# Loading the shifted replica in one transfer of 128 partitions, and laying out halves on even and odd partitions

## The reference, cut to what matters

```python
qkv = einsum('oc,bchw->bohw', w_qkv, x)                   # 256 -> 768 channels
y   = conv(qkv, w_dw, 5x5, pad 2, one group per channel)  # depthwise
agg = einsum('gok,bgkhw->bgohw', w_pw, y.reshape(B, 96, 8, H, W))
ms  = concatenate([qkv, agg], 1)                          # heads of 8 q, 8 k, 8 v channels
q, k = relu(...), relu(...)                               # v1: v with a row of ones appended
vk  = einsum('bhdn,bhen->bhde', v1, k)
out = einsum('bhde,bhen->bhdn', vk, q); out = out[:, :, :-1] / (out[:, :, -1:] + 1e-15)
out = einsum('oc,bchw->bohw', w_proj, out)
out = batchnorm(out) * gamma + beta + x                   # over all images and pixels
```

## Time and profile before

| | us |
|---|---|
| median of 3 runs | 2576.74 |
| lowest, highest | 2573.13, 2585.85 |
| the profiled execution | 2585.7 |
| its span | 2583.9 |

### The profile page before, as it was taken

The page is one execution under the profiler, slowest core; times in us unless marked ns, Lnnn a source line. Parts: engine busy times, 40 slices in busy tenths (PEclk is TensorE's granted clock), DMA queues, the critical chain, the costliest instruction groups (busy, mean ns, idle before and its releaser), DMA issues. The chain is left out here.

```text
span 2583.9 us, 36219 instructions
## 1 busy us (share of the span) xinstructions
PE 2282.2 (88%) x13760; PEld 1642.4 (64%) x13760; DVE 856.9 (33%) x1340; ACT 913.0 (35%) x1957; POOL 213.8 (8%) x207
## 2 busy tenths in 40 slices
PE   7999899996978999799979989998998999999730
PEld 6888888885755566566656656665665666666410
DVE  5666767665101221141123114112311411321352
ACT  4444344441333333323422333343233334333142
POOL 2222332221000000000000000000000000000000
PEclk9999999997989999899989999999998999999865
DMA  2111011103779877876877787687778758868668
GB/s 96 74 74 63 22 65 74 74 37 129 190 168 233 202 178 207 215 167 152 235 176 182 196 215 172 154 236 177 182 196 216 167 153 242 205 165 211 247 252 370
DMA packets 180737, 437.34 MB, mean 169 GB/s; under 512 B 7120, under 2 KB 155088, under 8 KB 162384
## 3 DMA queue, kind: packets, MB, share of 16 engines
q1 hardware_dynamic: 179408, 415.95, 59.8%
q0 software_dynamic: 1152, 18.87, 1.7%
HBM read 260.02 MB, written 174.78 MB: 168 GB/s over the span
## 5 line engine op out<-in xcount | busy, mean ns | idle before, releaser
L715 PE MATMUL cv<-work,wc 128*64 128x288 f32 x4608 | 632.6, 418 | 72.2 <-issue 59.6
L715 PEld LDWEIGHTS cv<-work,wc 128*64 128x64 f32 x4608 | 308.1, 138 | 312.5 <-issue 106.9
L1077 DVE TENSOR_TENSOR wc<-pwe,dwe 128x512 f32<-128x512 f32 x288 | 181.1, 686 | 881.8 <-PE cv L715 866.1
L696 PE MATMUL pj<-x,wqkv 128*128 128x288 f32 x1536 | 388.2, 409 | 22.2 <-DMA x<-scratch_x 22.2
L928 ACT ACTIVATE work<-cv 128x288 f32<-128x288 f32 x384 | 158.1, 412 | 600.4 <-PE cv L715 600.4
L696 PEld LDWEIGHTS pj<-x,wqkv 128*128 128x128 f32 x1536 | 289.5, 191 | 110.1 <-issue 35.5
L909 ACT COPY work<-pj 128x288 f32<-128x288 f32 x384 | 153.5, 400 | 289.7 <-PE pj L696 289.6
L753 PE MATMUL tr<-ident,work 128*128 128x128 f32 x1248 | 200.0, 285 | 16.8 <-issue 15.3
L732 PE MATMUL vk<-kvT 128*128 128x129 f32 x1248 | 202.7, 286 | 9.2 <-ACT kvT L945 4.9
L753 PEld LDWEIGHTS tr<-ident,work 128*128 128x128 f32 x1248 | 140.8, 144 | 99.0 <-issue 95.2
L732 PEld LDWEIGHTS vk<-kvT 128*128 128x128 f32 x1248 | 164.7, 192 | 24.6 <-ACT kvT L945 9.8
(11 more groups left out here) (104 smaller groups left out, 2882.1 us busy)
## 6 DMA issues: line engine op xcount, KB each, us to landing
scratch_padded<-work SPq DMA_DIRECT2D x48, 1300.0 KB, 4.5
work<-scratch_padded SPq DMA_DIRECT2D x48, 1300.0 KB, 9.4
work<-scratch_padded SPq DMA_DIRECT2D x48, 1296.0 KB, 15.4
scratch_phases<-work SPq DMA_DIRECT2D x96, 576.0 KB, 6.9
work<-scratch_phases SPq DMA_DIRECT2D x64, 576.0 KB, 6.0
x<-scratch_x SPq DMA_DIRECT2D x9, 2304.0 KB, 10.6
scratch_x<-xs SPq DMA_DIRECT2D x8, 2304.0 KB, 7.2
q<-scratch_phases SPq DMA_DIRECT2D x32, 576.0 KB, 5.7
```

Of the source, the lines that this page charges most:

```text
L696: mm = nc.tensor.matmul(pj[:, c % 2, :PLANE], wqkv[:, kc, u, :], x1[:, kc, c * PLANE:(c + 1) * PLANE], start=(kc == 0), stop=(kc == CT - 1))
L715: mm = nc.tensor.matmul(cv[64 * b:64 * b + 64, j % 2, :PLANE], wc[:, 2 * j + b, dy].rearrange("p c o -> p (c o)"), window, start=(dy == 0) ...
L1077: op = nc.vector.tensor_tensor(wc[:, blocks, dy], pwe[:, u, blocks].rearrange("p g (c o) -> p g c o", o=1).to_broadcast([P, HB, DIM, NG]), ...
```

## The change

`replicate` stores `padded` with the plane as the slowest axis (1024 pieces of 1300 bytes where 128 pieces of 10400 bytes were) and loads `rep` by a single transfer. For that the channels of `qpad` are ordered by position in the group first (`by_dim`), so that a row of `rep` is one run of 20.8 KB in memory; the partition of `rep` is (plane, channel position, shift), so that neighbouring partitions hold the same run, one value apart. `lay_out` writes its two halves to the even and the odd partitions. The constants follow: `mask8` and `headsel` get one version for each of the two channel orders (128 KB and 64 KB loaded where 64 KB and 32 KB were). No compute instruction is added or removed.

```diff
@@ -524,8 +524,8 @@
         dwe = sb("dwe", [P, NU, NB, KROWS, NG])
         wc = sb("wc", [P, NB, KROWS, DIM, NG])
         ident = sb("ident1", [P, P])
-        mask8 = sb("mask8", [P, P])
-        headsel = sb("headsel", [P, 2, 32])
+        mask8 = sb("mask8", [P, 2, P])
+        headsel = sb("headsel", [P, 2, 2, 32])
         spread = sb("spread", [P, 2, 4, P], F32R)
 
 
@@ -562,7 +562,7 @@
         NFIRST, NW = 3, 5
         last_image = NIMG - 1
         NDEN = NCH // 2
-        NREP, NLAY = 2 * 16, 16
+        NREP, NLAY = 16, 16
 
         Y_CHUNKS = {1: (0, 1), 2: (2, 3), 3: (4, 5)}
         SPREADS = {(0, 5): range(0, 2), (0, 6): range(2, 5), (0, 7): range(5, 8),
@@ -621,14 +621,14 @@
                 n = NU // 2 * i + u // 2
                 sp.wait_ge(pj_freed, i * (NU * NG) + (u + 1) * NG)
                 wait_count(sp, rep_in[u % 2], n * NREP)
-                sp.dma_start(dram["padded"][u % 2].rearrange("g (c l) n -> (g c) (l n)", c=DIM),
-                             qpad[:, u % 2, 0:NG * PADDED]).then_inc(padded_out[u % 2], 16)
+                sp.dma_start(dram["padded"][u % 2].rearrange("l p n -> p l n"),
+                             qpad[:, u % 2, 0:NG * PADDED].rearrange("p (l n) -> p l n", l=NG)
+                             ).then_inc(padded_out[u % 2], 16)
                 sp.wait_ge(padded_out[u % 2], (n + 1) * 16)
                 wait_count(sp, cv_filled, i * (NU * NG) + (u - 1) * NG)
-                for s in range(2):
-                    sp.dma_start(rep[64 * s:64 * s + 64, u % 2, 0:NB * PADDED].rearrange("p (g n) -> p g n", g=NB)[
-                        :, :, 0:PADDED - s], dram["padded"][u % 2].rearrange("g q n -> q g n")[:, :, s:PADDED]
-                    ).then_inc(rep_in[u % 2], 16)
+                rows = dram["padded"][u % 2]
+                sp.dma_start(rep[:, u % 2, 0:NB * PADDED - 1], bass.AP(
+                    rows.tensor, rows.offset, [[NB * PADDED, P // 2], [1, 2], [1, NB * PADDED - 1]])).then_inc(rep_in[u % 2], 16)
 
             def lay_out(i, u):
 
@@ -646,7 +646,7 @@
                     wait_count(sp, bn_done, 2 * NCH * i)
                 for h in range(2):
                     sp.wait_ge(lay_stored[h], laid_at(i, u))
-                    sp.dma_start(dst[64 * h:64 * h + 64], dram["phases"][4 * h:4 * h + 4].rearrange(
+                    sp.dma_start(dst[h:P:2], dram["phases"][4 * h:4 * h + 4].rearrange(
                         "j (k o) n -> (j k) (o n)", o=NG)).then_inc(lay_done[h], 16)
 
             def image(i, nxt):
@@ -1042,10 +1042,10 @@
                         pool.wait_ge(sa_filled, 4 * i + p - 1)
                     else:
                         wait_count(pool, sa_filled, 4 * i)
-                    nc.gpsimd.tensor_tensor(vkm[:, p % 2, :], vkraw[:, p % 2, 0:P], mask8[:], ALU.mult).then_inc(vkm_ready, 1)
+                    nc.gpsimd.tensor_tensor(vkm[:, p % 2, :], vkraw[:, p % 2, 0:P], mask8[:, PRODUCTS[p][1]], ALU.mult).then_inc(vkm_ready, 1)
                     wait_count(pool, den_filled, NDEN * i)
                     nc.gpsimd.tensor_tensor(dsel[:, slot_of(p)].rearrange("p e h -> p (e h)"),
-                                            headsel[:].rearrange("p e h -> p (e h)"),
+                                            headsel[:, PRODUCTS[p][1]].rearrange("p e h -> p (e h)"),
                                             vkraw[:, p % 2, P:P + 1].to_broadcast([P, 64]), ALU.mult
                                             ).then_inc(dsel_ready, 1)
 
@@ -1264,11 +1264,11 @@
 
     rows = np.array([[3 * DIM * h + DIM * PARTS[u] + d for h in range(16 * HALVES[u], 16 * HALVES[u] + 16)
                       for d in range(DIM)] for u in range(NU)])
-    wq = a["L1_conv_w_qkv"][rows]
+    by_dim = rows.reshape(NU, NB, DIM).transpose(0, 2, 1).reshape(NU, P)
+    wq = a["L1_conv_w_qkv"][by_dim]
     out["wqkv"] = wq.transpose(2, 0, 1).reshape(CT, P, NU, P).transpose(1, 0, 2, 3)
-    out["wproj"] = a["L1_conv_w_proj"].T.reshape(4, P, C).transpose(1, 0, 2)
     pw = a["L1_conv_w_pw"][rows[:, ::DIM] // DIM]
-    out["pwe"] = np.broadcast_to(pw.transpose(3, 0, 1, 2)[None, :, None], (2, DIM, NG, NU, NB, DIM)).reshape(P, NU, NB, DIM)
+    out["pwe"] = np.broadcast_to(pw.transpose(3, 0, 1, 2)[:, None], (NG, DIM, 2, NU, NB, DIM)).reshape(P, NU, NB, DIM)
     dw = a["L1_conv_w_dw"].reshape(-1, SCALE5, SCALE5)[rows].reshape(NU, NB, DIM, SCALE5, SCALE5)
     dwe = np.zeros((2, DIM, 2, 4, NU, NB, KROWS, 2, 4), dw.dtype)
     for s in range(2):
@@ -1280,19 +1280,21 @@
                             dy, dx = 2 * k + ry - r, 4 * s + xi - COLUMNS[xo]
                             if 0 <= dy < SCALE5 and 0 <= dx < SCALE5:
                                 dwe[s, :, ry, xi, :, :, k, r, xo] = dw[:, :, :, dy, dx].transpose(2, 0, 1)
-    out["dwe"] = dwe.reshape(P, NU, NB, KROWS, NG)
+    out["dwe"] = dwe.transpose(2, 3, 1, 0, 4, 5, 6, 7, 8).reshape(P, NU, NB, KROWS, NG)
     out["gb"] = np.stack([columns(a["L1_conv_bn_gamma"], CT), columns(a["L1_conv_bn_beta"], CT)], 1)
 
     k = np.arange(P)
     out["ident"] = np.eye(P, dtype=np.float32)
     out["mask32"] = (k[:, None] // HD0 == k[None] // HD0).astype(np.float32)
-    out["mask8"] = (k[:, None] // DIM == k[None] // DIM).astype(np.float32)
-    head = 16 * np.arange(2)[None, :, None] + k[:, None, None] // DIM
-    out["headsel"] = (head == np.arange(32)[None, None]).astype(np.float32)
+    group = np.stack([k % NB, 8 * (k % 2) + 2 * (k // 32) + k // 16 % 2])
+    place = DIM * group + np.stack([k // NB, k // 2 % DIM])
+    wproj = a["L1_conv_w_proj"].T.reshape(2, 2, P, C)
+    out["wproj"] = np.stack([wproj[s, h, place[s]] for s in range(2) for h in range(2)], 1)
+    out["mask8"] = (group.T[:, :, None] == group[None]).astype(np.float32)
+    out["headsel"] = (group.T[:, :, None, None] + NB * np.arange(2)[:, None] == np.arange(32)).astype(np.float32)
     j = np.arange(4)
-    row, half = k[:, None, None, None], 16 * np.arange(2)[None, :, None, None]
-    out["spread"] = ((row // 32 == j[None, None, :, None]) & (row % 32 == half + k[None, None, None] // DIM)
-                     ).astype(np.float32)
+    row, half = k[:, None, None, None], NB * np.arange(2)[None, :, None, None]
+    out["spread"] = ((row // 32 == j[None, None, :, None]) & (row % 32 == half + group[j // 2])).astype(np.float32)
     return {n: np.ascontiguousarray(v) for n, v in out.items()}
 
 
@@ -1308,7 +1310,7 @@
         dram[name] = nc.dram_tensor(f"in_{name}", a.shape, mybir.dt.from_np(a.dtype), kind="ExternalInput").ap()
     for name in ("x1", "y"):
         dram[name] = nc.dram_tensor(f"scratch_{name}", (NIMG, P, CT, HW), F32).ap()
-    dram["padded"] = nc.dram_tensor("scratch_padded", (2, NB, DIM * NG, PADDED), F32).ap()
+    dram["padded"] = nc.dram_tensor("scratch_padded", (2, NG, P, PADDED), F32).ap()
     dram["phases"] = nc.dram_tensor("scratch_phases", (NG, P, PLANE), F32).ap()
     dram["out"] = nc.dram_tensor("out_0", (NIMG, P, CT, HW), F32, kind="ExternalOutput").ap()
     build(nc, dram)
```

## The result

| | before | after |
|---|---|---|
| median, us | 2581.3 (4 runs) | 2547.2 (4 runs) |
| the profiled execution's span, us | 2583.9 | 2547.8 |
| ratio, with its 95% interval | | 0.9844 (0.9811 to 0.9878) |

By the ratio the change makes the kernel 1.6% faster (the two medians themselves lie 34.1 us apart, 1.3%); 2.4% was predicted. The ratio applied to the 2576.7 us from which the prediction started is 2536.5 us, outside the forecast's 2500 to 2530. That is close to the rival "the jumps don't shrink" (2542), but not for its reason, as will be seen: the jumps did shrink.

The account below looks back on a forecast made before the run. TensorE, busy 88%, was taken as the bound, with only its idle time and lost clock to win: 33.7 (image 0) + 27 (jumps) + 1.5 (end) - 0.5 (masks) = 61.7 us, from 2576.7 to 2515 us; forecast 2500 to 2530, whole range 2492 to 2548.

Parts of the forecast that it names:

- the jumps don't shrink: Layer 1's loop jumps: the code fetch waits as long as before, so 34.7 us won, 2542 us; chance 0.19.
- its own signs: Listed signs: `rep` load landing in 8 to 9 us, image 0's long waits gone, 4 to 8 us left at jumps.
- the three waits of image 0 that should be gone: TensorE's waits of 8.46 us for `rep` and of 7.82 and 7.46 us at the transposes were to vanish.
- The step from there to 8.0 us: Load of `rep`: 8 pieces for each engine make 6.4 us, plus 1.6 us of latency; 15.9 us before.
- The bound of 116 ns: Store of `padded` in 1300-byte pieces: upper price per piece, giving 7.4 us; 61 ns and 3.9 us were taken.
- the rival that ends slower: Store in 1300-byte pieces is slow and precedes the fetch at each jump; 2612 us at 230 ns a piece; chance 0.04.
- the quiet case: Layout loads (line 649) with nothing in the way: landing goes from 4.9 to about 3.6 us.
- the first step that failed: Image 0 and start of image 1: 27.9 us of waits plus 7.8 of clock, less 2 left, give 33.7 us.
- the second step that failed: Five jumps back of TensorE's loop in layer 1: from 11.9 to 6.5 us each, 27 us won.
- The rival of 4 us a jump: Layer 1's jumps: the fetch slips past or between the store's short pieces, 39.6 us won there, 2502 us; chance 0.12.
- The end and the masks: Image 7's denominators get the last layout 1.5 us sooner; larger masks at layer 1's start lose 0.5 us.
- The clock: TensorE's half clock after idle times: nothing was counted for it at the jumps; 7.8 us came back in image 0.

Follow-up runs that it names:

- two_halves: Changed kernel, but the replica loaded by two transfers, shift 0 into partitions 0 to 63, shift 1 into 64 to 127; 0.9949 of the kernel before.
- halves_only: Kernel before with only the layout loads going to even and odd partitions, replica load and store as they were; 0.9965 of the kernel before.

## Why the prediction was right, and where it was off

**The number.** 61.7 us were forecast, and the span shows 36.1. The whole range, 2492 to 2548, holds the measured time, but only because it takes in the rival of unchanged jumps, and the jumps did change; that is luck. By its own signs the forecast did badly: the load lands in 10.3 us and not 8 to 9, the jumps cost 9.3 us and not 4 to 8, and two of the three waits of image 0 that should be gone are still there.

**Where the time goes.** Right. The three places named (image 0, the jumps, the end) are those that got shorter. From image 1 on no other wait of TensorE shrank.

**The load of `rep`.** The step by which 704 ns for 18432 bytes becomes 794 ns for a piece holds: 775 ns were measured. The step from there to 8.0 us doesn't: it took eight pieces an engine at an even rate and 1.6 us of latency, and the transfer lands in 9.4 us at best and 10.3 in the median. I knew from the same issue list that 2304 KB to 128 partitions landed in 9.4 to 11.4 us, and should have set that landing against the packet price.

**The store in pieces.** 546 packets in 2 us at a share of 1.020 are 60 ns a piece, 61 predicted, 6.0 us to landing instead of 5.2. The bound of 116 ns and the rival that ends slower have nothing for them.

```profile
q1 hardware_dynamic: 546, 0.71, 102.0%
```

**Layout loads.** 3.9 us at best and 4.6 in the median, where 3.6 was predicted for the quiet case. The typical piece of 9216 bytes takes 347 ns instead of 688 (the medians of all such packets in layer 1). Right in kind.

**Image 0, the first step that failed.** The prediction let 2 us of waits stand and 10.3 stayed. The load's waits went wholly. The layout's didn't, since it takes part in a chain: replica load, then line 640's stores behind it (the first lands 11.1 us after its issue), then the layout loads. In the changed kernel SP and TensorE do this:

```profile
699.23 0.53 SPq L630 DMA_DIRECT2D work<-scratch_padded  x1
699.86 5.63 SPq L640 DMA_DIRECT2D scratch_phases<-work  x2
710.94 2.03 SPq L649 DMA_DIRECT2D work<-scratch_phases  x2
713.07 0.53 SPq L624 DMA_DIRECT2D scratch_padded<-work  x1
```

```profile
712.63 1.68 PE L715 MATMUL cv<-work,wc 128*64 128x288 f32 x12
719.48 0.87 PE L753 MATMUL tr<-ident,work 128*128 128x128 f32 x3 [5.17 <-issue]
```

The layout comes 14.5 us earlier than in the kernel before (719.5 against 733.95), but TensorE, which no longer waits for the replica, asks for it 11.8 us earlier (719.48 - 5.17 = 714.3 against 733.95 - 7.82 = 726.1). I subtracted both waits at full size, and the second starts from where the first ended. The term was 33.7 us; 12.6 + 5.0 us of waits and some 5 us of clock were measured, 23 us.

**The jumps, the second step that failed.** 6.5 us was taken and 9.3 measured; 27 us became 12.9. The mechanism was right, as holding back what is in line shows. Two of its terms were wrong: the layout loads were taken to be done at the jump, but with the load 2 us longer and two layout loads beside the store they weren't; and one fetch ahead of or behind the store was priced, where two follow each other and cost 5.8 us on idle engines. The rival of 4 us a jump was below what idle engines give and couldn't have come true. The second fetch comes when the data ahead of it are mostly out: after it 0.04 to 0.14 MB still start in the changed kernel. It starts 5.4 to 6.2 us after the first, against 3.1 to 3.4 with nothing in the way. The rule of the Trainium skill that each engine takes turns between its queues ("DMA: Bandwidth & Descriptors", Queues, rings and completion order) counts typically 9 to 17 pieces to a turn and at most 64. At 17 pieces a turn beside the new store would last 1 us (an estimate: 17 x 60 ns), less than this delay; at 64, an engine's whole share of the store, it would look like standing in line. So the waits seen here neither bear the rule out nor refute it.

**The end and the masks.** 1.0 us instead of 1.5 won at the end. The larger masks, for which 0.5 us was taken off, cost nothing that the trace shows: layer 1's first transposes wait 1.5 us for `spread` in both kernels.

**The clock.** I gave nothing for it at the jumps, and that was right: the first 5 or 6 us behind the jumps run at 0.51 to 0.60 in the changed kernel.

## What to carry to other kernels

Write a DMA's destination over all partitions, if need be by reordering channels: even and odd partitions do as well as one transfer of 128, and halves of 64 neighbours cost twice the time, with pieces of 9.2 KB as with 20.8 KB. When several waits lie on one chain, subtracting each at its full size counts the same microseconds twice; redo the chain with the new times and ask when the waiting engine will now be there. An idle time at a loop's jump that grows with the DMA work in line is a code fetch; write the loop out, or hold transfers that nobody needs yet until it is over.

## What of the hardware was not expected

- A jump of TensorE in layer 1 costs 5.8 us with no data on the DMA engines, more than twice the 2.65 us in layer 0, since it fetches two blocks one after the other, about 3 us apart. Writing out the loop of six images took 2.6% off the kernel before, more than the change itself.
- What the second fetch of a jump waits for hangs on a microsecond of SP's program. In the kernel before, four jumps cost 11.9 to 13.9 us and the one to image 4 costs 8.87. At the four, SP issues the store of line 624 1.4 to 1.8 us after the first fetch starts, and the second fetch starts 6.9 to 9.4 us after the first. At the cheap one SP issues it 2.9 us after the first fetch; the second starts within 0.6 us of that, ahead of the store's data. The issues there, and the queue from 1539.5 to 1540 us:

```profile
1535.54 3.55 SPq L649 DMA_DIRECT2D q<-scratch_phases  x2
1539.17 0.54 SPq L624 DMA_DIRECT2D scratch_padded<-work  x1
```

```profile
q8 instruction: 1, 0.02, 18.4%
```

- The same explains why each jump of `two_halves` costs 8.9 us, though its replica arrives as late as in `halves_only`, where a jump costs 10.6. In `two_halves` the store comes 2.8 to 3.3 us after the first fetch at all five jumps, and the second fetch starts 3.4 to 4.2 us after the first; in `halves_only` that is nearly so at one jump only (2.75 and 3.3 us), which costs 8.07 us. That one has the long pieces of 10400 bytes, so it isn't the short pieces that let the fetch through. This is read from the traces; no run shifts the store by so little. The jump to image 3 in `two_halves`:

```profile
1297.61 3.44 SPq L650 DMA_DIRECT2D q<-scratch_phases  x2
1301.14 0.54 SPq L624 DMA_DIRECT2D scratch_padded<-work  x1
```

```profile
1303.87 3.01 PE L716 MATMUL cv<-work,wc 128*64 128x288 f32 x12 [8.48 <-issue]
```
